# Where the score products of the first attention stand among the transposes

## The reference

```
q = jnp.einsum('nd,hdk->nhk', x, Wq) + bq        # 4 heads of 64
k = jnp.einsum('nd,hdk->nhk', x, Wk) + bk
v = jnp.einsum('nd,hdk->nhk', x, Wv) + bv
scores = jnp.sum(q[dst] * k[src], axis=-1) / np.sqrt(HEAD_DIM)
ex = jnp.exp(scores - seg_max[dst])
alpha = ex / (denom[dst] + 1e-16)
agg = jax.ops.segment_sum(alpha[:, :, None] * v[src], dst, num_segments=N)
```

## Time and profile before

| | us |
|---|---|
| median of 3 runs | 3530.02 |
| lowest, highest | 3528.23, 3532.93 |
| profiled execution | 3525.65 |
| its span, first to last instruction | 3524.0 |
| mean granted TensorE clock | 0.979 |

### The profile page before, as it was taken

How to read it: one execution, slowest core, us unless ns; L and a number is a source line. 1 busy time by engine, 2 the same in 40 slices (tenths; PEclk the granted TensorE clock), 3 DMA queues, 4 the chain that set the end, 5 groups by cost and what they waited for, 6 DMA issues and landing times. The chain is left out here.

```text
span 3524.0 us, 67249 instructions
## 1 busy us (share of the span) xinstructions
PE 3324.4 (94%) x25814; PEld 2694.6 (76%) x25815; DVE 2623.1 (74%) x4799; ACT 2078.5 (59%) x3840; POOL 652.2 (19%) x604
## 2 busy tenths in 40 slices
PE   5999997999999999997999999999899999999998
PEld 3555555888888888885777777777688888878887
DVE  8888885777767777766999999999599443236665
ACT  2555555777767767775999999999211111115454
POOL 1001000011111111111245236666100100000000
PEclk9999998999999999998999999999999999999999
DMA  2545558233333333426333533333666565553341
GB/s 83 222 193 218 217 212 262 94 113 124 107 106 130 106 106 106 131 85 203 107 114 112 193 109 106 132 106 113 219 222 222 194 213 191 205 211 140 133 149 58
DMA packets 202700, 534.72 MB, mean 152 GB/s; under 512 B 56881, under 2 KB 165462, under 8 KB 168502
## 3 DMA queue, kind: packets, MB, share of 16 engines
q1 hardware_dynamic: 199494, 526.25, 43.2%
q10 hardware_dynamic: 1904, 3.81, 0.4%
q0 software_dynamic: 1024, 0.82, 0.1%
HBM read 362.87 MB, written 167.80 MB: 151 GB/s over the span
## 5 line engine op out<-in xcount | busy, mean ns | idle before, releaser
L1141 PE MATMUL a_p_t<-ident,a_sm 128*128 128x128 f32 x5000 | 901.6, 279 | 33.3 <-ACT a_sm L1215 19.5
L1215 ACT ACTIVATE a_sm<-a_p_t 128x896 f32<-128x896 f32 (+3 forms) x800 | 668.4, 836 | 331.5 <-PE a_p_t L1141 286.3
L1209 ACT ACTIVATE a_sm<-a_sm,a_negm 128x896 f32<-128x896 f32 (+3 forms) x600 | 702.3, 1170 | 49.3 <-DVE a_negm L1272 49.0
L1141 PEld LDWEIGHTS a_p_t<-ident,a_sm 128*128 128x128 f32 x5000 | 616.5, 142 | 144.6 <-issue 113.4
L1168 PE MATMUL a_p_o<-a_sm,a_v 128*64 128x128 f32 x10000 | 701.8, 279 | 16.5 <-ACT a_sumT L1222 16.3
L1300 DVE CUSTOM_DVE_ANT_0 a_sm<-a_p_s,sh_rows 128x400 f32<-128x400 f32 x790 | 439.9, 571 | 288.8 <-PE a_p_s L1123 253.2
L1168 PEld LDWEIGHTS a_p_o<-a_sm,a_v 128*64 128x64 f32 x10000 | 557.2, 137 | 122.0 <-issue 73.1
L1123 PE MATMUL a_p_s<-sh_kt,sh_q 128*128 128x400 f32 x1580 | 588.2, 432 | 34.4 <-DVE a_mx L1300 19.9
L1123 PEld LDWEIGHTS a_p_s<-sh_kt,sh_q 128*128 128x128 f32 x1580 | 305.4, 194 | 58.4 <-DVE a_mx L1300 29.4
L1321 DVE SCALAR_TENSOR_TENSOR a_sm<-sh_wide,sh_al 128x3125 f32<-128x3125 f32 x100 | 346.8, 3468 | 4.1 <-PEq L54 2.4
L1331 DVE CUSTOM_DVE_ANT_0 a_sm<-a_sm,sh_rows 128x3125 f32<-128x3125 f32 x100 | 348.5, 3485 | 1.0
(11 more groups left out here) (319 smaller groups left out, 4873.4 us busy)
## 6 DMA issues: line engine op xcount, KB each, us to landing
sh_rows<-d_full SPq DMA_DIRECT2D x67, 1600.0 KB, 7.0
sh_ct<-d_ct SPq DMA_DIRECT2D x50, 1600.0 KB, 6.6
d_ct<-sh_wide SPq DMA_DIRECT2D x25, 1600.0 KB, 5.3
d_full<-sh_rows SPq DMA_DIRECT2D x25, 1600.0 KB, 5.8
t_third<-d_ct SPq DMA_DIRECT2D x25, 1600.0 KB, 6.7
d_logs<-sh_rows SPq DMA_DIRECT2D x23, 1664.0 KB, 6.0
sh_rows<-d_logs SPq DMA_DIRECT2D x23, 1664.0 KB
sh_q<-d_q SPq DMA_DIRECT2D x200, 64.0 KB, 2.3
```

What stands on the lines that cost most here:

```text
L1141: m = nc.tensor.transpose(p_t[u % 2][:, i * P:(i + 1) * P], sm[buf][:, a * P:(a + 1) * P], ident[:, :])
L1209: nc.scalar.activation(sm[buf][:, c], sm[buf][:, c], ACT.Exp, bias=negm[:, buf:buf + 1], accum_out=parts[:, buf, e:e + 1]).then_inc(s_prob, 1)
L1215: nc.scalar.activation(sm[buf][:, a_row[u] * P:a_row[u + 1] * P], p_t[u % 2][:, 0:turns[u] * P], ACT.Copy).then_inc(s_copy, 1)
```

## The change

`turn_and_score` issues all transposes of a slot, and then the four score products in one run. Slots of 7 become T T T T T T T S S S S and slots of 4 T T T T S S S S. No instruction is added or removed, and all waits stay with the instruction that they stood at. The second attention has no score products (`dot` is false), and its order stays as it was.

```
                     later = ahead(at, 2) if dot else None
-                    blocks, parts, done = turns[u] if exists(at) else 0, 0 if later is None else SCORE_PARTS, 0
-                    for i in range(blocks):
+                    for i in range(turns[u] if exists(at) else 0):
                         turn_block(at, u, i)
-                        while done < parts and (done + 1) * (blocks + 1) <= (i + 1) * (parts + 1):
-                            score_part(later, u, done)
-                            done += 1
-                    for m in range(done, parts):
+                    for m in range(0 if later is None else SCORE_PARTS):
                         score_part(later, u, m)
```

## The result

| | before | after |
|---|---|---|
| median us, 6 runs each | 3529.91 | 3505.90 |
| lowest, highest | 3523.37, 3532.93 | 3497.20, 3511.37 |
| profiled execution, its span | 3525.65, 3524.0 | 3507.07, 3505.4 |

The ratio is 0.9932, 95% interval 0.9917 to 0.9947: 24 us faster by the medians, 18.6 by the two spans. Forecast were 13.5 us faster, at 3516.5.

A forecast was written before the change was run, and what follows sets the result against it. PE was taken to bound the first attention (977 of 1007 us busy). Savings of 7, 6 and 0.5 us in its waits sum to 13.5, taking the 3530.0 median to 3516.5 us; own range 3508 to 3523, 8-in-10 range 3502 to 3530.

The forecast's parts named there:

- the 0.44: PE's wait at a tile's second head, first slot, for DVE's mask; expected to give way to two of about 0.13.
- The stream: PE's products and transposes in the first attention: a product costs 0.184 us whichever its neighbour; zero gain, bounds -20 to +7.
- rival A: A run of score products streams at 169 ns each, giving 18 us more: 3498 us; chance 0.07.
- The signals: ACT's copy is released 0.55 us earlier in slots of 7, worth nothing; score blocks complete later, banks are wanted later.
- Wait 1: PE's regular wait for masks, mainly at the second head's first slot: 0.57 us per tile falls to 0.25; -7 us.
- Wait 3: PE's single 7.9 us wait for keys at the second unit; five more transposes hide in it, -0.5 us.
- Wait 2: Irregular PE stops around the third head, from late PE-DVE signals: later bank requests save 6 us, bounds +6 to -12.
- New waits: PE waiting for the second bank where slots 1 and 2 follow directly: no cost expected, but thin.
- rival C: Slower by the second bank: masks 0.13 us longer under product runs, 20 us lost, 3536 us; chance 0.08.
- the margin of 0.06: Slot 2 after slot 1: second bank lets the product stream at 2.57 us, wanted at 2.63; no cost.
- Rival D: Runs of up to seven transposes let TensorE fall to 1.2 GHz, about 3567 us; chance 0.03.
- Rival B: Nothing measurable: irregular stops save nothing or worsen by 6, regular wait gives its lower bound; about 3525 us, chance 0.27.

The follow-up runs named there:

- the pair without stops: Kernel before and changed kernel, each with the scattered store of source terms replaced by 8 whole rows of the identity matrix: 3501.3 and 3490.2 us.
- the second traces: Unedited repeats for another trace: the kernel before on the third chip, 3557.6 us (one run); the changed kernel on the second, 3531.1 us, ratio 0.9910.
- even_slots: Against the kernel before: score products in a run of four in slots 0 and 2 only, old spread in 1 and 3; 3538.0 us, ratio 0.9929.

## Why the prediction was right

The direction and the mechanism of the regular wait were right, and the measured 3505.9 lies in the range for 8 in 10 (3502 to 3530). It lies 2 us below the forecast's own narrower range (3508 to 3523). Of the signs named beforehand, the runs of four at 0.18, the two waits of about 0.13 in place of the 0.44 and the sum under 20 us came; the stage became 18.6 us shorter and not 13, the waits for DVE did not become more (31 for 34), and ACT's wait for transposes did change, by 30 us, at no cost to PE.

**The stream**: zero taken, 2.4 us saved. Product behind product is 183 ns, so rival A (169) is out; the saving is inside the bounds I gave, and the 0.184 from one warm pair was right to 1 ns. **The signals**: ACT's earlier release is worth nothing, as said; PE's wait for it is 2.9 for 2.7.

**Wait 1**: forecast -7, bounds -12 to -2; measured 7.8 in the first pair of traces (11.2 to 3.4) and 7.7 in the pair without stops. The two waits left over came at 0.11 and 0.13 us for 0.13 and 0.12. What I had wrong is only that six tiles more have none, since 14 of 25 have it instead of 20.

**Wait 3**: forecast 0.5, measured 2.4 in the DMA's row; the load's landing varies, as the first two units show (6.4 to 9.8 us over all traces, both orders; in the pair without stops the change has the longer one, 9.1 for 7.0). So 2 of these 2.4 us are luck.

**Wait 2 is the term that was mis-sized**: forecast -6, bounds +6 to -12. By the medians it is about 13 (24.0 with stops on the first chip, 11.1 without on the fourth), by the stages of the two first traces 25.0 - 16.9 = 8.1, by those of the second traces 52.8 - 34.8 = 18.0. The step I had wrong is that only waits in front of score products count. By these alone the first traces would give 20.9 - 10.7 = 10.2; but 2.9 of it came back as stops in front of the value products, and the lower clock behind the stops, a term I had put at nothing although shows its product of 0.70, cost 4.0 us before and 3.3 after. Also, I took the late signals as given. They were 10 us less in the profile after than in the profile before for DVE, and the same for ACT (29 for 30 us). So how much of the 8 to 18 us is the order, as I had worked it out, and how much is that the signals happened to be less late, these traces don't tell; that -6 lies near the first pair is in part luck. Whether the order makes the signals less late is open too: on the second and third chips DVE's were 46.5 after and 59.6 before, but even_slots had 62.2.

**New waits, rival C**: in slots 1 and 2 side by side the margin of 0.06 held; past the first two units no wait at slot 2 of the first, second and fourth head in the change's traces, and masks take 0.56 to 0.58. **Rival D**: 0.99 granted in the stage, with runs of seven transposes in all of it; what fell to the lower level in it, behind the first units, fell behind stops of PE, and without stops nothing did. By the Trainium skill (TensorE: Matmul & The Clock Gate, Part 4: PE-mode transpose) transposes should not keep the clock up; no run here shows a loss from them in this mix. **Rival B**: out, interval and cause both.

**The statement on the cause of the stops** ("while SP issues the next queries' eight DMAs") was right in time and only half right as a hint: the stops need the scattered store issued before them, and the loads add to their cost.

## What to carry to other kernels

With a ring of two banks between two engines, an order pays or costs by two clocks: when a bank is asked for, and when its successor's block is complete. Asking later behind a busy consumer gains (slots 0 and 2), completing later in front of an early request loses (slots 1 and 3, +18.6 us); work each slot from the rows rather than trust "grouped" or "spread". And where waits of one place vary in size for no reason on the engines, look at what the DMA queue just started: one small store of single numbers cost this kernel 30 to 40 us on engines that never touch it. Before a gain of a few microseconds is measured, such stops have to go: they moved equal kernels by up to 30 us. And a stop's price is the whole stage's, not the wait's alone.

## What the runs showed of the hardware

- A DMA of 128 x 8 scattered four-byte numbers, 23 times, made PE's signals to DVE up to 5.8 us late, 27 to 62 us in sum in nine traces, 0.5 us in the five without it. PE's signals to ACT were late by 29 to 57 us in sum in the same nine, and never by over 0.25 us in the five. How it does so stays open.
- Behind a stop of 3.2 us PE's granted clock was 0.50 for the next 6.7 us (before, 1011.60 to 1018.30). Such stretches cost the stage most of 3 to 12 us on top of the stops.
- A 400-column product costs 183 ns behind its like at the 2.4 GHz level, where the lower level has 333, exactly 400 columns at 1.2 GHz. Half of 333 would be 167; what the other 16 are was not tried.
- A bank freed by DVE reaches PE's weight load 0.05 us later and the stream 0.11 after that: 0.16 us for each hand-over that is waited for.
